# Scoring the experts' router with x as the stationary operand, in float32, instead of the router as the stationary operand

## The reference, cut to what matters

```python
logits = jnp.einsum('btd,de->bte', x, Wr)          # Wr is 512 x 8
inhibition = jax.nn.sigmoid(logits / temperature)
in_zone = (inhibition >= GOLDEN_LOWER) & (inhibition <= GOLDEN_UPPER)
distance = jnp.abs(inhibition - GOLDEN_CENTER)
w = jnp.exp(-distance / 0.1) * in_zone.astype(x.dtype)
...
out = jnp.einsum('ebtf,efd->ebtd', mid, Wd)
...
return jnp.einsum('bte,ebtd->btd', weights, out)
```

## Time and profile before

| | us |
|---|---|
| median of 3 runs (lowest to highest) | 2358.25 (2356.95 to 2360.74) |
| the profiled execution | 2356.86 |
| its span, first to last instruction | 2355.1 |
| PE busy | 2267.4 (96%) |
| DVE busy | 1575.6 (67%) |
| ACT busy | 889.1 |
| POOL busy | 758.4 |

### The profile page before, as it was taken

One profiled execution on the slowest core, in us unless ns is written; L12 is line 12 of the kernel. 1 busy time (PEld: TensorE's weight loads), 2 busy tenths in 40 slices (PEclk: granted clock), 3 DMA queues, 4 the chain that ended last, 5 costly groups with the idle time before them and its releaser, 6 DMA issues.

```text
span 2355.1 us, 30907 instructions
## 1 busy us (share of the span) xinstructions
PE 2267.4 (96%) x10746; PEld 1861.6 (79%) x10746; DVE 1575.6 (67%) x2392; ACT 889.1 (38%) x1441; POOL 758.4 (32%) x570
## 2 busy tenths in 40 slices
PE   8899999999989999999999899999999899999997
PEld 6787788888867888888877688777778778888885
DVE  5557777777758855674455666667677886777665
ACT  4456333333334322322232444234344444444441
POOL 0002544444412222341111533224233543333331
PEclk9999999999999999999999999999999999999998
DMA  5646222222132100000000211221111021111110
GB/s 205 218 141 201 63 72 71 71 71 71 55 110 100 36 19 19 23 1 19 1 1 27 81 53 56 81 81 61 47 54 54 27 90 54 53 54 53 53 36 36
DMA packets 90567, 154.36 MB, mean 66 GB/s; under 512 B 6224, under 2 KB 55376, under 8 KB 83808
## 3 DMA queue, kind: packets, MB, share of 16 engines
q1 hardware_dynamic: 90464, 153.02, 19.4%
HBM read 113.68 MB, written 39.32 MB: 65 GB/s over the span
## 4 chain that ended last, share of the span: by engine, by line
PE 61%; DVE 6%; issue 2%; ACT 1%; POOL 1%; DMA 0%; POOLq 0%; DVEq 0%; ACTq 0%; SPq 0%
PE attn_pvk L1197 4%; PE attn_pvk L1199 4%; PE attn_pvk L1198 4%; PE attn_pq L1197 2%; PE attn_pq L1198 2%; PE attn_pq L1199 2%; PE attn_pv L1197 2%; PE attn_po L1197 2%; PE attn_po L1198 2%; PE attn_po L1199 2%; PE attn_pv L1199 2%; PE attn_pv L1198 2%; PE attn_pv L85 2%; PE attn_pv L87 2%; PE attn_pv L86 2%
## 5 line engine op out<-in xcount | busy, mean ns | idle before, releaser
L2570 DVE TENSOR_TENSOR moe_a_lo<-moe_up_raw,moe_a_hi 128x512 fp32r<-128x512 f32 x192 | 182.7, 967 | 154.8 <-ACT moe_a_hi L2033 154.7
L1915 POOL TENSOR_TENSOR moe_h_lo<-moe_c_t,moe_h_hi 128x512 fp32r<-128x512 f32 x96 | 128.3, 1336 | 356.8 <-ACT moe_h_hi L2033 356.7
L1197 PE MATMUL attn_pvk<-moe_b_hi,moe_a_hi 128*128 128x512 f32 x512 | 200.8, 392 | 13.8 <-ACT moe_c_last L2159 5.8
L1199 PE MATMUL attn_pvk<-moe_b_hi,moe_a_lo 128*128 128x512 f32 x512 | 199.4, 389 | 0.0
L1198 PE MATMUL attn_pvk<-moe_b_lo,moe_a_hi 128*128 128x512 f32 x512 | 199.3, 389 | 0.0
L2033 ACT ACTIVATE moe_c_t<-attn_pvk 128x512 f32<-128x512 f32 x192 | 113.2, 596 | 186.5 <-PE attn_pvk L1199 184.5
L1305 POOL TENSOR_TENSOR ffn_h_lo<-ffn_h_f,ffn_h_hi 128x512 fp32r<-128x512 f32 x64 | 89.9, 1405 | 254.1 <-ACT ffn_h_hi L1360 254.1
L2085 ACT ACTIVATE moe_c_t<-moe_c_t 128x512 f32<-128x512 f32 x96 | 60.4, 629 | 241.6 <-DVE moe_c_t L2642 241.6
L1507 DVE SCALAR_TENSOR_TENSOR all_acc<-attn_pvk,ffn_wts,all_acc 128x512 f32<-128x512 f32 x128 | 91.2, 749 | 89.0 <-PE attn_pvk L87 88.8
L2033 ACT ACTIVATE moe_a_hi<-moe_up_raw 128x512 fp32r<-128x512 f32 x192 | 116.0, 624 | 56.4 <-POOL moe_up_raw L1885 56.4
L1197 PEld LDWEIGHTS attn_pvk<-moe_b_hi,moe_a_hi 128*128 128x128 f32 x512 | 96.2, 188 | 37.6 <-issue 11.0
(11 more groups left out here) (497 smaller groups left out, 6564.4 us busy)
## 6 DMA issues: line engine op xcount, KB each, us to landing
moe_up_raw<-in_e_up SPq DMA_DIRECT2D x28, 1024.0 KB, 5.8
moe_dn_raw<-in_e_dn SPq DMA_DIRECT2D x28, 512.0 KB, 3.7
xh<-mix_out_hi SPq DMA_DIRECT2D x32, 256.0 KB, 2.6
zs<-mix_out_z SPq DMA_DIRECT2D x32, 256.0 KB, 3.2
xl<-mix_out_lo SPq DMA_DIRECT2D x32, 256.0 KB, 3.4
mix_x<-xh SPq DMA_DIRECT2D x16, 512.0 KB, 4.2
mix_x<-xl SPq DMA_DIRECT2D x16, 512.0 KB, 5.3
mix_z_raw<-zs SPq DMA_DIRECT2D x16, 512.0 KB, 3.9
```

The costliest lines, as they stand in the source:

```text
L1197: pe.matmul(out, lh, rh, start=first, stop=False, skip_group_check=True)
L1199: return pe.matmul(out, ll, rh, start=False, stop=True, skip_group_check=True)
L1915: tt(h_lo[:, m, tok], src, raw(h_hi[:, m, tok]), ALU.subtract).then_inc(s_hlo, 1)
L2570: tt_(a_lo[q][:], src, raw(a_hi[q][:]), ALU.subtract).then_inc(s_alo, 1)
```

## The change

x becomes the stationary operand and the router the moving one: for each of the eight chunks of a pair, four float32 matmuls with a part of turned x (128 x 128) loaded and 8 columns of the router streamed, all into one bank, with the tokens on partitions at once. The scoring of the first pair is one block in chunk 12 (`SCORED_AT`), that of the second pair one block in slot 11, ahead of its first down product. The parts of the router (`rw`), the copies of logits (`logits_copy`, `first_log`, `log_t`) and `turn_logits` are gone. The bank is taken by one DVE copy each time; in chunk 12 it stands in DVE's order between `low_out` and `low_x`, and PE waits for it (`s_lgt`) before `turn_x`. POOL's first difference of x waits for the logits (`s_wts`).

```diff
-            def logits(bank, b):
-                for kt in range(KT):
-                    ins = pe.matmul(bank[0:NE], rw_raw[:, kt], xr[:, kt, bass.ts(b, SEQ)], start=kt == 0, stop=kt == KT - 1)
-                return ins
-
-            def logits_of_parts(bank):
...
-            def turn_logits(bank, log_t, parts=False):
+            def logits(bank, sem):
+
                 for c in range(PC):
...
+                    for kt in range(KT):
+                        ins = pe.matmul(bank[:, c * NE:(c + 1) * NE], xr[:, kt, bass.ts(c, P)], rw_raw[:, kt],
+                                        start=c == 0 and kt == 0, stop=kt == KT - 1, skip_group_check=True)
+                ins.then_inc(sem, 1)
...
# PE, extras of slot 11
-                if at(n, SCORING) and c < 2:
-                    if c == 0:
-                        pe.wait_ge(s_free, ring_of(SCORING))
-                    logits(ring.bank(), c).then_inc(s_ring, 1)
-                if at(n, SCORING) and c == 2:
-                    pe.wait_ge(s_free, ring_of(SCORING) + 3)
-                    turn_logits(ring.bank(), log_t).then_inc(s_ring, 1)
+                if at(n, SCORING) and c == 0:
+                    pe.wait_ge(s_free, ring_of(SCORING))
+                    logits(ring.bank(), s_ring)
...
# PE, chunk(n)
-                if n == TOKENS_AT:
-                    pe.wait_ge(s_lgc, 2)
-                    turn_logits(pt[:], first_log, True).then_inc(s_wts, 1)
...
-                if n == PARTS_AT:
-                    pe.wait_ge(s_xr, turns[-1] + 1)
-                    pe.wait_ge(s_rwlo, 1)
-                    pe.wait_ge(s_blo, 2)
-                    logits_of_parts(pt[:]).then_inc(s_lg, 1)
-                if n == PLAIN_AT:
+                if n == SCORED_AT:
+                    pe.wait_ge(s_small, 32)
                     pe.wait_ge(s_xr, PC)
-                    logits(pt[:], 1).then_inc(s_lg, 1)
+                    logits(pt[:], s_wts)
...
-                    if n == PARTS_AT:
-                        pe.wait_ge(s_lgc, 1)
-                    if n == PLAIN_AT:
-                        pe.wait_ge(s_lgc, 2)
-                    if n == TOKENS_AT:
+                    if n == SCORED_AT:
                         pe.wait_ge(s_lgt, 1)
                     turn_x(n + 1)
...
# DVE, chunk(n)
                 if n == TOKENS_AT:
-                    dve.wait_ge(s_wts, 1)
-                    link(nc.vector.tensor_copy(wts[:, 0:PC], on_tokens(pt[:])[:, :, 0:NE]))
-                    tt_(wts[:, 0:CPB], wts[:, 0:CPB], on_tokens(pt[:])[:, 0:CPB, NE:2 * NE], ALU.add).then_inc(s_lgt, 1)
                     dve.wait_ge(s_lgt, 1)
                     router(0, 0)
...
+                if n == SCORED_AT:
+                    dve.wait_ge(s_wts, 1)
+                    nc.vector.tensor_copy(wts[:, 0:PC], on_tokens(pt[:])).then_inc(s_lgt, 1)
                 if n < NCH - 1:
                     low_x(n + 1)
...
# POOL, x_sums
                     if pair == 0:
-                        pool.wait_ge(s_xr, PC)
+                        pool.wait_ge(s_wts, 1)
...
                 if part == 2:
-                    pool.wait_ge(s_lg, 2)
                     tt(b12, b22, b12, ALU.subtract).then_inc(s_bsum, 1)
```

More of the change, by code:

```diff
@@ L1591, in ffn_attn_experts @@
         AHEAD = {8: (0, 1), 9: (2, 3), 10: (4, 5), 11: (6,), 12: (7,)}
-        PARTS_AT, PLAIN_AT, TOKENS_AT = 11, 12, 13
+        SCORED_AT, TOKENS_AT = 12, 13
         w_pos = pos - 4 * KT * 3 * DM
@@ L1655, in ffn_attn_experts @@
         rw_raw = at_m.sb("rw_raw", [P, KT, NE])
-        rw = at_m.sb("rw", [P, KT, 2 * NE], F32R)
         rb = at_m.sb("rb", [P, 1])
@@ L1663, in ffn_attn_experts @@
         first_cmp = [scratch[:, i * DM:(i + 1) * DM].rearrange("p (c i j) -> p c i j", c=PC, i=NE) for i in (0, 1)]
-        first_log = [scratch[0:2 * NE, i * DM:(i + 1) * DM] for i in (2, 3)]
         xrf = xr[:].rearrange("p k n -> p (k n)")
@@ L1667, in ffn_attn_experts @@
                                       for i in range(4))
-        log_t = (c_last[0:2 * NE], cmp_2[0:NE].rearrange("p c i j -> p (c i j)"))
         block_a = lambda par, m, kh: up_raw[:, par, :, m, 2 * kh:2 * kh + 2, :]
@@ L1703, in ffn_attn_experts @@
         s_et, s_xr = k.sem("x_turned"), k.sem("x_turned_ready")
-        s_lg, s_lgc, s_lgt, s_wts = (k.sem(n) for n in ("logits_summed", "logits_copied", "logits_on_tokens",
-                                                      "logits_turned"))
+        s_wts, s_lgt = k.sem("logits_summed"), k.sem("logits_taken")
         s_router = k.sem("ranks_taken")
-        s_rwhi, s_rwlo = k.sem("router_hi_ready"), k.sem("router_lo_ready")
         s_z, s_e = k.sem("router_to_act"), k.sem("router_from_act")
@@ L1735, in ring_of @@
             known = (0, 0, 8, 16, 24, 32, 46, 60, 74, 88, 96, 112)
-            return known[n] if isinstance(n, int) and n < 12 else 8 * n + 27
+            return known[n] if isinstance(n, int) and n < 12 else 8 * n + 25
         def slots(eng, slot):
@@ L1758, in extra @@
             if at(n, SCORING):
-                return (1, 2, 3, 3, 3, 3, 3, 3)[c]
+                return 1
             return 0
@@ L1991, in ahead_x @@
                                      ACT.Copy).then_inc(s_xr, 1)
[L1993 to L1996, removed]
             def chunk(n):
@@ L2018, in chunk @@
                     ahead_x(turns[1])
-                if n == PARTS_AT:
-                    logits_copy(0)
-                if n == PLAIN_AT:
-                    logits_copy(1)
                 if n == TOKENS_AT:
@@ L2171, in _ @@
                     up_high(0, 0, 0, 1)
-                    act.wait_ge(s_small, 32)
-                    copy(rw[:, :, 0:NE], rw_raw[:]).then_inc(s_rwhi, 1)
                 if n == 9:
@@ L2626, in extras @@
                     nc.vector.tensor_copy(xr[:, c % KT, bass.ts(c // KT, SEQ)], bank).then_inc(s_free, 1)
-                if at(n, SCORING) and c < 2:
+                if at(n, SCORING) and c == 0:
                     bank = ring.bank()
[L2629 to L2633, removed]
+                    nc.vector.tensor_copy(wts[:, PC:NCH], on_tokens(bank)).then_inc(s_free, 1)
                     dve.wait_ge(s_free, ring.base + ring.off)
-            on_tokens = lambda bank: bank[:, 0:PC * 2 * NE].rearrange("p (c e) -> p c e", c=PC)
+            on_tokens = lambda bank: bank[:, 0:PC * NE].rearrange("p (c e) -> p c e", c=PC)
             def combine(n, i, tile, bank, q, got, sem):
@@ L2817, in _ @@
                     up_low(0, 0, 1)
-                    dve.wait_ge(s_rwhi, 1)
-                    tt_(rw[:, :, NE:2 * NE], rw_raw[:], raw(rw[:, :, 0:NE]), ALU.subtract).then_inc(s_rwlo, 1)
                 if n == 9:
```

## The result

The changed kernel takes 2368.89 us (median of 5, 2366.70 to 2370.52) against 2358.25 (median of 5, 2355.50 to 2360.74) of the kernel before: 1.004 times the time, interval 1.0028 to 1.0051. That is 10.6 us slower, about twice the 0.2% that can be told from no change. The forecast was 2359.8 with a range up to 2367.0, so the result lies on the side of rival 1, and 1.9 us above the range. The profiled execution took 2369.1 us, with a span of 2367.4.

A forecast was written before the change was run, and what follows sets the result against it. PE, busy 96% of the span, was taken as the bound. PE's balance of -0.21 us plus a new wait of 1.75 made +1.5 us, 2359.8 us from a median of 2358.25; range 2356.5 to 2367.0.

The forecast's parts named there:

- rival 1: In the new blocks, loads that hardly stream let PE's clock fall: 2363.2 to 2366.6 us, bound 2370.2; chance 0.38.
- The mixer's row: Evidence from the mixer before the change: 3.4 us of loads with 64 columns kept the granted clock at 1.00.
- 0.78: First pair, PE's own balance: 7.22 us for chunk 12's block less 6.44 us of removed work, +0.78 us.
- -0.99: Second pair in slot 11, PE's own balance: 7.23 us for the block less 8.22 us removed, -0.99 us.
- The pitch of 0.11 us a load: In both new blocks each 128-column float32 load sets 0.11 us, so 64 make a block of 7.04 us.
- The cost of the block in its place: Block with gap ahead and restart behind: 7.22 us in chunk 12, 7.23 us in slot 11.
- The new wait ahead of `turn_x`: In chunk 12 PE waits for DVE's late logits copy to free bank `pt`: +1.75 us, bounds 1.5 to 2.2.
- the bound of 1.3: End of slot 11: possible PE wait for the last product, taken as 0, with 1.3 us kept as a bound.
- ACT, DVE and POOL at 0: Work saved or delayed on these three engines costs 0, as PE's own work hides it.
- Rival 2: Both blocks load at the small transposes' pace, 0.074 us each, saving 4.6 us: 2355.2 us; chance 0.05.
- Rival 3: In chunk 12 DVE's copy gets in ahead of earlier work, so PE's wait vanishes: 2358.0 us; chance 0.07.
- the balance of -0.21 us: PE's own work over both pairs, added less removed: -0.21 us, so swapping operands saves next to nothing.

The follow-up runs named there:

- e1: Changed kernel with 64 columns instead of 8 streamed behind each load, in both blocks; 2357.48 us, 1.0001 of before.
- e4: Changed kernel's 8 columns, but each pair's loads cut into pieces between dense work, and no wait for the logits ahead of `turn_x`; 2357.44 us, 0.9996 of before.
- e2: As e1, with DVE's copy of chunk 12's logits moved ahead, right behind its division; 2357.81 us, 0.9995 of before.
- e5: Changed kernel with 8 columns, DVE's copy of chunk 12's logits moved right behind its division; 2365.57 us, 1.0037 of before.
- e8: Changed kernel with 64 columns in chunk 12 and slot 11's 8-column block split into two of 32 records; 2361.05 us, 1.0013 of before.
- e6: Changed kernel with 16 columns instead of 8 behind each load, in both blocks; 2370.05 us, 1.0055 of before.
- e7: Changed kernel with 32 columns instead of 8 behind each load, in both blocks; 2365.70 us, 1.0041 of before.
- e3: Changed kernel with 64 columns in slot 11 only, 8 kept in chunk 12; 2365.97 us, 1.0028 of before.

## Why the prediction was wrong

**The step that failed** is the choice between forecast and rival 1, and there this sentence: "Against it: 3.4 us of loads with 64 columns, half of the time without a stream, kept 1.00, and PE was never out of instructions there." Both halves misled. The mixer's row speaks for a block with 64 columns, and e1 bears it out to the letter, twice over in length; it says nothing of 8 columns, with which the same loads fall. And that PE has instructions all the time isn't enough: in the changed kernel's falls it was never without one. The sum was therefore made at 1.00 throughout, and the clock's term, which was the largest, had weight only as a rival with a chance of 0.38. What speaks for the rival, "no stretch of the trace is so poor in columns for so long", was the better argument. The rule of the Trainium skill beside it ("TensorE: Matmul & The Clock Gate", "Part 1: The HAM clock gate") goes by how busy PE has been. In these traces a matmul in flight all the time was not enough: a block of 64 float32 loads with 8, 16 or 32 columns each fell to 0.50, and one with 64 columns kept 1.00.

**The size of that term was too small as well.** Rival 1 took the lengths of the falls from before's trace, 3.4 and 6.9 us, and got 1.7 to 3.4 us lost for each. They last 10.2 us in the changed kernel, 5.1 lost each, and 13.7 or 6.8 in other runs. Its bound, "up to half a block, 3.5 us", + 1.7 = 5.2 for each, was right in size, and its cause, loads at half speed, is what the blocks show: 0.21 us a record in place of 0.11. The forecast's +1.5 with two falls of 5.1 would have been +11.7; measured is +10.6. By place it is 0.78 + 1.75 + 5.1 = 7.6 in chunk 12, where the profile has 7.3, and -0.99 + 5.1 = 4.1 in slot 11, where it has 3.9. It was the range that didn't follow the bound: it ended at 2367.0, with the bound at 2370.2.

**The terms of the forecast were right** wherever the clock was up:

- The pitch of 0.11 us a load, and the block of 7.04: 7.07 and 7.06 in e1, 0.107 in e4.
- The cost of the block in its place, forecast 7.22 in chunk 12 and 7.23 in slot 11. In e1 it is 1236.99 - 1229.49 = 7.50 from the q turnings, whose row begins 0.43 ahead of the block, less the 0.35 of a chunk without scoring: 7.15. In slot 11 it is 1682.69 - 1675.40 = 7.29 from L1199, less 0.23, plus 0.09 for the late restart behind it: 7.15.
- The new wait ahead of `turn_x`: forecast +1.75 (1.5 to 2.2). It is 2.19 - 0.44 = 1.75 in the changed kernel and in e1, and gone in e2 and e5. As it was said, DVE's copy waits in program order behind the copy of the values and `low_out`.
- No PE wait for a last product at the end of slot 11; the one at the end of slot 12 stayed what it was, as the list of waits of the changed kernel for that stretch shows, so the bound of 1.3 wasn't used:

```profile
PE attn_pvk L1197 <- DVE moe_c_last L2691: 1.3, 1, 1.3
```

- ACT, DVE and POOL at 0: their busy times moved by 0.3 to 2.8 us, and behind neither block does PE wait for them, except for the DVE copy ahead of `turn_x`.

**The other rivals.** Rival 2, quick loads at 0.074, is false in every run: plain float32 loads don't reach the pace of the small transposes. Rival 3, the change without the wait, is false as the change stands; e5 and e2 make it by moving the copy, and show that it is worth its 1.75 us in the timeline and nothing that these medians can tell.

**What stays open.** Why a fall lasts 6.8, 10.2 or 13.7 us isn't shown. The profiled executions have one order in it: the more of the block was left when the clock fell, the longer the fall. With 0.7 and 1.9 us of the block left (e8) it lasted 6.8 us, with 5.5 to 7.4 left 10.2 (chunk 12 of the changed kernel, slot 11 of it and of e5, e6 and e7), with 8.0 to 8.6 left 13.7 (chunk 12 of e3, e5, e6 and e7). This was read off afterwards, and no run tested it. If it holds, e5's 13.7 needs no part of the early copy. No version that was tried beats the kernel before: e1, e2 and e4 are level with it, since the swap of operands itself saves next to nothing, as the balance of -0.21 us said.

## What to carry to other kernels

Swapping operands so that the long side becomes the weight turns a matmul that streams into one that only loads; price it by the load, and then ask what the granted clock does in such a stretch and in the work behind it, for the engine may be busy all through and still be given half speed. Where such loads are needed, spread them between products that stream (16 records at a time cost nothing here, 32 at a time let the clock fall) or, where the bank has room, put more columns behind each. And when a rival's worst case is worked out with the right mechanism, let the range reach it.

## What the hardware showed that I had not expected

- A matmul instruction in flight all the time doesn't keep PE's clock: with 8, 16 or 32 columns behind each 128x128 float32 load, all nine profiled blocks of 64 records fell from 1.00 to 0.50, 2.6 to 4.2 us after their start; with 64 columns behind each none of six did.
- At the lower level a float32 load takes 0.21 us in place of 0.11, so a block of loads pays for a fall in full.
- The falls came in three lengths, 6.8, 10.2 to 10.3, and 13.7 us, and went on into the products behind the block. In e8's profiled execution two blocks of 32 records lost 6.8 us together, where one block of 64 lost 5.1; over all its executions the loss was smaller.
- At the upper level the pace of these loads doesn't depend on the columns behind them, from 8 (0.107 us) to 64 (0.110 us).
